# Key tables without constant rows: four key transfers per load instead of one

## The reference

```python
x = x + jnp.tanh(g_xattn[l]) * xattn_l(_layernorm(x), ctx_1024, ...)
x = x + jnp.tanh(g_ffn[l]) * ffn_l(_layernorm(x), ...)
```

```python
scores = einsum("bhqd,bhkd->bhqk", q, k) / sqrt(8)
attn = softmax(scores)            # layer 0: times a gate per key; layer 3: some keys masked
out = einsum("bhqk,bhkd->bhqd", attn, v)
```

## Time and profile before

| | |
|---|---|
| median of 3 runs | 1746.88 us (1746.49 to 1747.47) |
| profiled execution, own time | 1748.62 us |
| its span | 1746.9 us |
| PE, DVE, ACT busy | 88%, 75%, 67% |
| HBM read and written | 85.05 MB and 34.23 MB |
| mean granted PE clock | 0.893 |
| attention of layer 0 begins (first score matmul) | 74.26 us |
| local run of layer 1, first and last maxima issued | 435.30 and 529.93 us |

### The profile page before, as it was taken

How to read it: one execution, slowest core, us unless ns; L and a number is a source line. 1 busy time by engine, 2 the same in 40 slices (tenths; PEclk the granted TensorE clock), 3 DMA queues, 4 the chain that set the end, 5 groups by cost and what they waited for, 6 DMA issues and landing times.

```text
span 1746.9 us, 46570 instructions
## 1 busy us (share of the span) xinstructions
PE 1541.6 (88%) x15481; PEld 656.9 (38%) x15481; DVE 1313.9 (75%) x2284; ACT 1167.7 (67%) x2209; POOL 147.0 (8%) x242
## 2 busy tenths in 40 slices
PE   5699999977776999997798699999878999999967
PEld 4423333355112333333575333333353444444345
DVE  6599999356446999992686699999347888888258
ACT  3269999732441889895596289999643777777636
POOL 5000000012000000000231000000010000000012
PEclk9689999988555999998698799999986999999879
DMA  9821212106111121210020611221152111111001
GB/s 272 272 63 55 63 54 63 49 0 198 37 36 56 54 61 55 63 54 25 25 86 18 204 53 54 63 63 53 39 150 73 56 42 53 42 52 33 24 13 37
DMA packets 90147, 120.66 MB, mean 69 GB/s; under 512 B 20823, under 2 KB 62318, under 8 KB 90062
## 3 DMA queue, kind: packets, MB, share of 16 engines
q1 hardware_dynamic: 86686, 110.63, 21.4%
q0 software_dynamic: 2432, 7.94, 1.4%
q10 hardware_dynamic: 944, 0.93, 0.2%
HBM read 85.05 MB, written 34.23 MB: 68 GB/s over the span
## 4 chain that ended last, share of the span: by engine, by line
PE 64%; DVE 17%; issue 8%; DMA 4%; SPq 4%; ACT 2%; POOL 1%; DVEq 0%; ACTq 0%; POOLq 0%
PE pv_bank L1494 22%; DVE mx L1044 12%; PE exp_ring L1482 11%; PE score_ring L1456 6%; PE exp_ring L1474 4%; PE score_ring L1452 4%; PE score_ring L1671 3%; PE exp_ring L1682 3%; PE exp_ring L1479 3%; DMA qp<-ms 2%; DMA k_d<-k2c 2%; PE score_ring L1377 1%; PE exp_ring L1384 1%; PE score_ring L1584 1%; ACT early L818 1%
## 5 line engine op out<-in xcount | busy, mean ns | idle before, releaser
L818 ACT ACTIVATE early<-exp_ring 128x512 f32<-128x512 f32 (+1 forms) x1728 | 920.5, 599 | 281.0 <-PE exp_ring L1482 162.6
L1044 DVE TENSOR_REDUCE mx<-score_ring 128x2 f32<-128x802 f32 (+2 forms) x832 | 743.9, 962 | 65.6 <-PE score_ring L1456 65.4
L1494 PE MATMUL pv_bank<-early,vg 128*32 128x256 f32 (+1 forms) x6912 | 562.2, 404 | 0.7 <-issue 0.2
L1456 PE MATMUL score_ring<-kp,qp 64*128 64x400 f16 (+2 forms) x1664 | 347.5, 359 | 45.9 <-DVE mx L1044 37.3
L1482 PE MATMUL exp_ring<-qp,kp 64*128 64x512 f16 (+1 forms) x1312 | 347.8, 401 | 35.5 <-DMA qp<-ms 33.0
L1494 PEld LDWEIGHTS pv_bank<-early,vg 128*32 128x32 f32 (+1 forms) x6912 | 145.6, 109 | 254.7 <-issue 130.5
L1482 PEld LDWEIGHTS exp_ring<-qp,kp 64*128 64x128 f16 (+1 forms) x1312 | 101.4, 95 | 240.8 <-ACT early L818 164.1
L1456 PEld LDWEIGHTS score_ring<-kp,qp 64*128 64x128 f16 x1664 | 84.1, 95 | 220.1 <-DVE mx L1044 185.1
L1452 PE MATMUL score_ring<-kp,qp 64*64 64x400 f16 (+1 forms) x1024 | 137.6, 356 | 12.5 <-DVE mx L1037 8.8
L1474 PE MATMUL exp_ring<-qp,kp 64*64 64x512 f16 x832 | 129.7, 399 | 2.8 <-DMA qp<-ms 2.8
L1479 PE MATMUL exp_ring<-ctxT,mask_eye 64*64 64x512 f16 x800 | 125.8, 384 | 0.0
(11 more groups left out here) (242 smaller groups left out, 1354.0 us busy)
## 6 DMA issues: line engine op xcount, KB each, us to landing
kp<-k_d SPq DMA_DIRECT2D x128, 400.2 KB
k_d<-k1c SPq DMA_DIRECT2D x32, 400.2 KB, 6.7
qp<-q_d SPq DMA_DIRECT2D x640, 12.0 KB
ctxT<-ctxT_d SPq DMA_DIRECT2D x12, 800.5 KB, 6.0
k_d<-k2c SPq DMA_DIRECT2D x16, 400.2 KB, 7.4
k_d<-v_loc POOLq DMA_DIRECT2D x12, 400.2 KB, 8.7
ctxT_d<-ctxT SPq DMA_DIRECT2D x4, 800.5 KB, 7.1
o_all<-in_ctx SPq DMA_DIRECT2D x4, 768.0 KB
```

What stands on the lines that cost most here:

```text
L818: act.activation(pt[g][0:rows_, 2 * h:2 * h + 2, :], bank[0:rows_, :].rearrange("p (i q) -> p i q", q=S), ACT.Exp).then_inc(exped, 1)
L1044: dve.tensor_reduce(dst, src, AX.X, ALU.max).then_inc(score_free, 1)
L1456: ins = pe.matmul(pa[slot][:, z, 0:w], qp1[par][rows_, i, qt * P:qt * P + P], kp1[par][rows_, at:at + w], start=True, stop=True)
L1494: ins = pe.matmul(po[R * j:R * j + R, 0:S], vg[par][0:rows_, s, j, :], pt[g][0:rows_, j, :], start=(s == 0), stop=(s == r.kt - 1))
```

## The change

The eight rows of ones are no longer in the DRAM tables. The writes of them and their waits go. Instead POOL sets the four key buffers to ones over all 128 partitions, once, at the start, each when its earlier contents have been read; SP waits for the four before the first key load. From then on a key load writes only the 24 data rows of each head, in four transfers, each issued ahead of the query transfer of the same head. The counts that PE waits for grow from 5 to 8 transfers per pass.

```diff
-IN_DMAS = 16 * (1 + HG) // 2
+IN_DMAS = 16 * 2 * HG // 2
...
-            def constant_rows(r):
-
-                for b in range(B):
-                    sp.dma_start(k_d[r.index][4 * b:4 * b + 4].rearrange("g (i r) n -> (g i) r n", r=R)[:, KQ:R, :],
-                                 one16[:, 0:r.nk]).then_inc(padded0, 16)
...
                 if r.layer == 0:
-                    sp.wait_ge(dconst, 4)
-                    constant_rows(r)
                     ctx_load(2)
...
                         if r.layer == 0:
-                            sp.wait_ge(padded0, 16 * B)
                             sp.wait_ge(dconst, 9)
-                            sp.wait_ge(prep_w, 10)
-                            sp.wait_ge(prep_v, 11)
+                            sp.wait_ge(ones_ok, 4)
                         if r.layer == 1:
-                            sp.wait_ge(padded, 16 * B * (len(RUNS) - 1))
                             sp.wait_ge(lk_out, 16 * 12)
...
             def pass1(r, n, par):
-                sp.dma_start(kp1[par][:, 0:r.nk], k_d[r.index][n]).then_inc(in1[par], 16)
                 for i in range(HG):
+                    sp.dma_start(kp1[par][R * i:R * i + KQ, 0:r.nk], k_d[r.index][n, R * i:R * i + KQ, :]
+                                 ).then_inc(in1[par], 16)
                     sp.dma_start(qp1[par][R * i:R * i + KQ, i, :], q_d[r.layer][n, R * i:R * i + KQ, :]
                                  ).then_inc(in1[par], 16)
...
             def pass2(r, n, par):
-                sp.dma_start(kp2[par][:, 0:r.nk], k_d[r.index][n]).then_inc(in2[par], 16)
                 for i in range(HG):
+                    sp.dma_start(kp2[par][R * i:R * i + KQ, 0:r.nk], k_d[r.index][n, R * i:R * i + KQ, :]
+                                 ).then_inc(in2[par], 16)
...
-                    pool.wait_ge(dconst, 4)
-                    for r in RUNS[1:]:
-                        for b in range(B):
-                            pool.dma_start(
-                                k_d[r.index][4 * b:4 * b + 4].rearrange("g (i r) n -> (g i) r n", r=R)[:, KQ:R, :],
-                                one16[:, 0:r.nk]).then_inc(padded, 16)
-                    pool.wait_ge(prep_v, 3)
+                    pool.wait_ge(prep_w, 10)
+                    pool.memset(kp1[0][:, 0:S2], 1.0).then_inc(ones_ok, 1)
+                    pool.memset(kp2[0][:, 0:S2], 1.0).then_inc(ones_ok, 1)
+                    pool.wait_ge(prep_v, 1)
+                    pool.memset(kp2[1][:, 0:S2], 1.0).then_inc(ones_ok, 1)
+                    pool.wait_ge(prep_v, 11)
+                    pool.memset(kp1[1][:, 0:S2], 1.0).then_inc(ones_ok, 1)
...
             def local_split():
-                dve.wait_ge(padded, 16 * B * (len(RUNS) - 1))
```

More of the change, by code:

```diff
@@ L331, in flamingo @@
         dconst = sem("dconst")
-        padded0, padded = sem("padded0"), sem("padded")
+        ones_ok = sem("ones_ok")
         w_turned, w_kept = sem("w_turned"), sem("w_kept")
```

## The result

| | median (lowest to highest) | runs |
|---|---|---|
| before, on the same chip | 1747.18 us (1746.49 to 1748.33) | 4 |
| after | 1796.49 us (1796.18 to 1798.54) | 4 |

The ratio is 1.0284 [1.0266, 1.0302]: 49 us slower, where 53 were forecast. The profiled execution of after took 1798.54 us, its span is 1796.8 (before: 1746.9).

What follows compares the result with a forecast made beforehand. The prediction took SP's issue queue as the local run's pace and, in long runs, how late the maxima may come before PE stands. Terms -6 + 38 + 1.7 + 19 = +53 us on 1747 gave 1800 us, range 1767 to 1828.

Steps and rivals of the forecast that it cites:

- The local run: Layer 1's attention with 256 keys, at SP's pace: six more issues per unit paid in full, +38 us (24.5 to 45.4).
- the first loads: Three static loads in `loads_start` ahead of the local run: nine more issues, partly hidden, +1.7 us (0 to 3.7).
- The plain long runs: Three unmasked runs of 1601 keys: maxima 1.44 us later, PE stands 0.46 longer in 42 units, +19 us (0 to 29).
- the cover: Plain long runs: maxima may be 0.98 us late before PE stands; beyond it delay is paid one for one.
- That one pair of units: Long-run units beginning at 1045.48 and 1076.41: maxima 1.22 us late cost 0.24, which gave the cover of 0.98.
- The masked run: Layer 3: 1.5 us more cover than the plain run, so the 1.44 us delay is hidden, 0 us.
- The start: Before attention: 20 constant-row transfers gone, so the first context store comes earlier, -6 us (4 to 7.5 gained).
- up to 2.75 more: The start: eight key matmuls took 5.71 us after idling, 2.96 later; up to 2.75 us gained beyond 4.5.
- The memset wait: The start: POOL's four memsets of ones over by 52, so SP's new wait for them costs nothing.
- Only the local run pays: Rival: extra slots shrink to 0.303, long-run delay of 0.91 stays under the cover; +20, 1767 us; chance 0.22 (1765 to 1786).
- The maxima also travel later: Rival: slots of 0.56, maxima land 0.3 us later behind key rows; +85, 1832 us; chance 0.17 (1816 to 1835).
- Faster: Rival: a 24-row issue takes time in proportion to its rows, 0.07 us; 1745 to 1747, down to 1740; chance 0.06.

Runs made afterwards that it cites:

- local split: Kernel before, key loads in four transfers of 24 rows in layer 1's local run alone, both passes: 1777.82 us, ratio 1.0178.
- the last run: Kernel before, constant rows later, local run's pass 2 loads issued by POOL as soon as the buffer is free, pass 1 still ahead of the maxima: 1737.64 us.
- The kernel with the maxima first: Changed kernel, SP issuing a unit's maxima ahead of pass 1 of the unit after next, not behind it: 1774.24 us, 1.0166.
- the split of all loads: Kernel before, every key load of both passes and all runs in four transfers of 32 rows: 1811.70 us, 1.0384.
- pass 1 alone split: Kernel before, only pass 1 of the four long runs loading keys in four transfers of 32 rows: 1773.99 us, 1.0156.
- late: Kernel before, local run's pass 2 loads issued by POOL behind its copy of the values, not by SP: 1797.84 us, 1.0297.
- the first one with pass 2 on POOL: Changed kernel with maxima first, local run's pass 2 loads issued by POOL behind its copy of the values: 1808.74 us, 1.0369.

## Why the prediction was right

**The local run (+38, and 1.7 for the first loads).** Right in mechanism and nearly in sum: +37.4. The local split alone shows it (8.86 us a unit), and that SP's issues were part of the pace shows in the last run, where five fewer gave 0.8 us a unit back. The parts were sized otherwise. Six issues added 2.36 us to a unit, 0.39 each, not 2.81 (pass 1 1.12, forecast 1.46; pass 2 1.24, forecast 1.35): 31.0 between first and last maxima. The nine static loads put off the run's first pass 1 in a unit by 3.0 us (435.80, before 432.26, less the 0.5 of layer 0), towards the top of their bounds, and that pass 1 took 1.5 more; and another `loads_start`, that of the next run, stands in the last 1.9, which the prediction had not counted. The units of 9.1 to 9.4 us were a little too long: 8.82 in the mean.

**The plain long runs (+19).** Measured 20.4, and the terms hold: the maxima are 1.40 us later (forecast 1.44), PE waits 0.43 to 0.46 us at the first fill (0.46), and the cover is 0.94 to 0.97 (0.98). That one pair of units gave it so nearly was in part luck: it was read from the length of the unit, and by PE's wait of 0.33 us that pair has 1.22 - 0.33 = 0.89. Off is the count: 12 waits a run, not 14, 17.7 us in all three. The remaining 2.7 us are growth without a wait, which the prediction did not have. The kernel with the maxima first proves the cause: the growth is gone. That the data of pass 1 and pass 2 hide behind the unit is shown by the same run and by the split of all loads (16.0 us with or without pass 2).

**The masked run (0).** Right, in after (19.41 us against 19.38 a unit) and with pass 1 alone split (19.44).

**The start (-6).** Right in size for the two profiles (-6.3) and in the path: in after ACT waits for PE and no longer for the context store, PE's key matmuls begin 3.5 us earlier (53.19, before 56.67; forecast 52.1), and the eight take 2.96 us instead of 5.71, the forecast's "up to 2.75 more" in full.

```profile
51.44 1.57 ACT L734 ACTIVATE ctxT<-exp_ring 128x512 f32<-128x512 f32 x3 [0.88 <-PE exp_ring L1298]
53.19 2.96 PE L1367 MATMUL score_ring<-ctxT,wsq 128*128 128x401 f32 x8 [0.92 <-ACT ctxT L734]
```

That second part is the clock: while those eight ran, the granted clock was 0.50 in before (the lower level, 1.2 GHz; PE had stood 5.04 us) and 1.00 in after. That SP's four transfers were the cause is not shown, only that the twenty were. Over all profiles, attention starts at 63.7 to 69.0 us in the four kernels without them (mean 66.5) and at 74.0 to 75.4 in the ten with them (74.7), so the gain may be nearer 8.

**The memset wait (nothing).** Right in cost, wrong in time. The last memset ended at 55.76, not 52, and SP did stand at it:

```profile
SPq L444 <- POOL kp L664: 8.4, 1, 8.4
```

The first key load left at 55.91; attention began at 67.99 behind PE's own key and value matmuls, so nobody waited for SP. The 16 issues that had to be out by then were out by 63.1.

**The rivals.** "Only the local run pays" falls with the waits in the plain runs. "The maxima also travel later" falls too: from the end of their issue to PE's fill it is 1.03 us in after (1112.45 to 1113.48) and 1.05 in before (1050.39 to 1051.44). "Faster" needed an issue whose length goes with its rows, 0.07 us for 24. The median is 0.303 and half the rows of a full load cost more than all of them, so neither size nor bytes set it. The Trainium skill's sentence that initiating a DMA is usually small relative to the DMA ("DMA: Bandwidth & Descriptors", "Issuing engines are not separate DMA queues") gives the wrong side here for the local run: with pass 1 first, what was initiated, and by whom, was worth 31 us (the local split), -10 (pass 2 issued by POOL early) and 51 (late).

## What to carry to other kernels

Before a transfer is split to move less, count the issues of the queue that carries it per unit of work, and look for what stands behind them: three issues of 24 rows ahead of a small urgent transfer cost more than the 128 rows they replaced. A delay ahead of a covered transfer costs no wait until the cover is used up and is then paid one for one; read it from the waits and from the length of the units, which here grew by a little more. Issues can be given to an idle engine, but then the place in that engine's order decides: behind a wait for the previous unit's end they are worse than on the crowded queue.

## What the runs showed of the hardware that was not expected

The length of a load's issue on SP does not grow with its rows: 0.303 us for 24 rows, 0.32 to 0.34 for 32, 0.485 to 0.558 for 64, 0.36 for 128. An issue of POOL in a loop takes 0.50 to 0.55 us.

A short DVE instruction was held up beside POOL's memsets of 128 x 1601. The row of DVE before and the two engines after: 0.19 us became 3.47, and the instruction ended (49.66) as the third of the memsets in a row did (49.62).

```profile
43.66 0.19 DVE L934 TENSOR_SCALAR gate_e<-gate_e 128x52 f32<-128x52 f32 x1 [0.31 <-ACT gate_e L723]
```

```profile
45.44 1.44 POOL L659 MEMSET kp<- 128x1601 f16 x1 [26.64 <-DVE early L919]
46.19 3.47 DVE L925 TENSOR_SCALAR gate_e<-gate_e 128x52 f32<-128x52 f32 x1 [0.31 <-ACT gate_e L714]
46.81 1.44 POOL L660 MEMSET kp<- 128x1601 f16 x1
48.18 1.44 POOL L662 MEMSET kp<- 128x1601 f16 x1
54.32 1.44 POOL L664 MEMSET kp<- 128x1601 f16 x1 [4.71 <-DVE mask_add L937]
```

Three other kernels with these memsets show the same (3.47 to 3.48 us). In the first one with pass 2 on POOL the instruction stood beside one memset only, 0.73 us, and the third memset took 3.12. The Trainium skill ("SBUF — State Buffer", "SBUF: two separate sides") has DVE, in a mode that uses two ports, and GpSimd share one pair of ports, which the one that starts first holds for its whole instruction while the other stands; the rows agree in kind, but no run shows DVE's mode, and in four of five profiles the DVE instruction stood through three of POOL's in a row, 3.3 us. That is part of why the memsets ended at 55.76: the mask's conversion ended at 54.26, 5.8 us later than the 48.45 of the forecast, 3.3 of it by this hold, 2.5 because DVE's work ahead of it was late already.
